# Routing weights normalised where they are gathered: a change to a transformer layer on one core

## What is computed

```python
x = x + 0.5 * ffn(layernorm(x))
x = x + attention(layernorm(x))
x = x + 0.5 * ffn(layernorm(x))

# in ffn: 2048 tokens, 64 experts, K = 4 of them per token, 32 slots per expert
logits = flat @ router_w.T
scores = softmax(logits)
_, topk_idx = top_k(logits + router_bias, K)
topk_w = take_along_axis(scores, topk_idx)
topk_w = topk_w / topk_w.sum(axis=-1, keepdims=True)
# tok_table, w_table: the first 32 tokens that chose each expert, and their weights
xg = flat[tok_table]
y = down(silu(gate(xg)) * up(xg))
out = zeros.at[tok_table].add(y * w_table)     # plus a shared expert of width 512
```

## Time and profile before

| | us |
|---|---|
| time, median of 3 runs | 971.72 |
| lowest and highest | 968.83, 972.66 |
| span of the profiled execution | 969.0 |
| TensorE busy | 918.5 (95%) |
| VectorE busy | 764.3 (79%) |
| ScalarE busy | 647.1 (67%) |
| GpSimd busy | 645.5 (67%) |

### The profile page before, as it was taken

One profiled execution on the slowest core, in us unless ns is written; L12 is line 12 of the kernel. 1 busy time (PEld: TensorE's weight loads), 2 busy tenths in 40 slices (PEclk: granted clock), 3 DMA queues, 4 the chain that ended last, 5 costly groups with the idle time before them and its releaser, 6 DMA issues.

```text
span 969.0 us, 18581 instructions
## 1 busy us (share of the span) xinstructions
PE 918.5 (95%) x5809; PEld 559.7 (58%) x5812; DVE 764.3 (79%) x2079; ACT 647.1 (67%) x1426; POOL 645.5 (67%) x607
## 2 busy tenths in 40 slices
PE   7989888999999999999999999999999999977987
PEld 4766465555555555555555555555555555765666
DVE  6954399998888888888888888888878789876247
ACT  5624546887777687777778778777777787643431
POOL 3367778878576868778676766867677455336642
PEclk9999999999999999999999999999999999989999
DMA  8979745566766878797885755756675574485657
GB/s 335 367 243 314 265 170 164 108 132 113 144 132 104 157 158 186 153 211 162 175 192 98 154 107 133 153 104 138 108 153 93 93 117 91 80 334 170 244 204 274
DMA packets 302978, 165.58 MB, mean 171 GB/s; under 512 B 278176, under 2 KB 285600, under 8 KB 300832
## 3 DMA queue, kind: packets, MB, share of 16 engines
q1 hardware_dynamic: 297696, 146.56, 62.8%
q0 software_dynamic: 3072, 9.44, 3.0%
q10 hardware_dynamic: 2112, 8.39, 2.2%
HBM read 68.93 MB, written 28.31 MB: 100 GB/s over the span
## 4 chain that ended last, share of the span: by engine, by line
PE 75%; DVE 13%; issue 4%; DMA 3%; ACT 3%; POOL 1%; SPq 0%; another core or an unknown queue 0%; ACTq 0%; DVEq 0%; POOLq 0%
PE b_o L110 5%; PE b_o L112 5%; PE b_o L111 5%; PE b_p L110 5%; PE b_s L110 5%; PE b_s L112 5%; PE b_s L111 5%; PE b_p L111 5%; PE b_p L112 5%; PE b_out L110 3%; PE b_out L112 3%; PE b_out L111 3%; PE b_v L110 2%; PE b_v L112 2%; PE b_v L111 2%
## 5 line engine op out<-in xcount | busy, mean ns | idle before, releaser
L2460 POOL TENSOR_TENSOR h<-pr,h 128x512 f16<-128x512 f32 x256 | 293.0, 1157 | 159.9 <-ACT h L1179 154.2
L1169 ACT ACTIVATE pr<-b_s,nmax,kappa 128x512 f32<-128x512 f32 x256 | 197.6, 774 | 42.2 <-DVE nmax L1915 37.0
L1912 DVE TENSOR_SCALAR_CACHE_REDUCE junk<-b_s 128x512 bf16<-128x512 f32 x256 | 175.3, 685 | 22.6 <-PE b_s L112 17.5
L1179 ACT ACTIVATE h<-pr 128x512 f16<-128x512 f32 x256 | 153.2, 626 | 0.8 <-DMA pT<-h 0.4
L1943 DVE SCALAR_TENSOR_TENSOR x<-b_out,rinv,x 128x256 f32<-128x256 f32 x256 | 111.4, 476 | 41.7 <-PE b_out L112 40.2
L110 PE MATMUL b_p<-xh,w 128*128 128x512 f16 x256 | 97.0, 379 | 4.3 <-DVE qT L1854 2.6
L110 PE MATMUL b_o<-pT,v 128*128 128x512 f16 x256 | 97.0, 379 | 1.7 <-DVE oT L1931 1.7
L110 PE MATMUL b_s<-kT,qT 128*128 128x512 f16 x256 | 97.0, 379 | 0.7 <-ACT pr L1169 0.7
L112 PE MATMUL b_s<-kT,qT 128*128 128x512 f16 x256 | 97.0, 379 | 0.0
L111 PE MATMUL b_s<-kT,qT 128*128 128x512 f16 x256 | 97.0, 379 | 0.0
L111 PE MATMUL b_o<-pT,v 128*128 128x512 f16 x256 | 97.0, 379 | 0.0
(11 more groups left out here) (225 smaller groups left out, 2236.6 us busy)
## 6 DMA issues: line engine op xcount, KB each, us to landing
raw<-in_experts SPq DMA_DIRECT2D x32, 768.0 KB, 7.2
raw_cs<-in_heads SPq DMA_DIRECT2D x16, 1024.0 KB, 5.1
zrows<-zero ACTq DMA_DIRECT2D x4, 2048.0 KB, 11.6
z<-zrows SPq DMA_DIRECT2D x16, 512.0 KB, 4.2
zrows<-zero SPq DMA_DIRECT2D x16, 512.0 KB, 4.0
zl<-zrows SPq DMA_DIRECT2D x16, 512.0 KB, 10.5
rows<-xn SPq DMA_DIRECT2D x8, 512.0 KB, 12.1
pT<-h SPq DMA_TRANSPOSE x256, 3.2
```

The source lines that it names most:

```text
L1169: act.activation(pr[n % 4][:], b_s[n % 3][:], ACT.Exp, bias=nmax[:, u % 2, i:i + 1], scale=kappa[:, s:s + 1], accum_out=rsum[:, u % 2, i:i ...
L1179: act.activation(h[n % 4][:, 0, :], pr[n % 4][:], ACT.Copy).then_inc(q["p_high"], 1)
L1912: dve.tensor_scalar(junk[n % 2][:], b_s[n % 3][:], 0.0, None, ALU.add, ALU.max, accum_out=peaks[:, n % 2:n % 2 + 1]).then_inc(q["peak_read ...
L2460: pool.tensor_tensor(h[n % 4][:, 1, :], pr[n % 4][:], h[n % 4][:, 0, :], ALU.subtract).then_inc(q["p_split"], 1)
```

## The change

The store of the weights follows the masked product at once: `sum_weights` and `weighted` are gone, with `esum` and `rsum_w`, two of the semaphores, and their places in the lists of VectorE and GpSimd. `slot_weights`, called once for each of the 32 groups, adds up all 64 gathered weights of each row (`whole`), takes the reciprocal (`fraction`), and multiplies the slot's own weight (`part`) by it. Three instructions on 128 rows are added to each call, with one more wait.

```diff
--- before.py
+++ after.py
@@ -148,8 +148,8 @@
         nmr = m.keep("nmr", [P, NT])
         best = m.keep("best", [P, NT, 8])
         mx = m.keep("mx", [P, NT])
-        esum = m.keep("esum", [P, NT])
-        rsum_w = m.keep("rsum_w", [P, NT])
+        whole, fraction = m.keep("whole", [P, NG]), m.keep("fraction", [P, NG])
+        part = m.keep("part", [P, NG])
         first = m.keep("first", [P, CAP])
         cand = m.keep("cand", [E, 2 * CAP])
         top = m.keep("top", [E, CAP])
@@ -235,7 +235,7 @@
         ctx.enter_context(nc.psum_tensor("all_banks", [P, 8 * 512], F32))
 
         names = ("consts p_hi p_lo veps_ready rstd_ready nmr_ready xn_ready xt_turned hi_done lo_done "
-                 "lgT_done lgT_sb pick_ready lg_done sh_done exp_done_w masked sum_ready w_ready w_out mask_ready maskT_done maskT_sb kidx_done keys_done "
+                 "lgT_done lgT_sb pick_ready lg_done sh_done exp_done_w w_ready w_out mask_ready maskT_done maskT_sb kidx_done keys_done "
                  "first_done cand_done top_done tab_done idx_ready gu_done sil_done hid_ready hhi_done hlo_done down_done x_added "
                  "turned sb_x act_done esil_done ehid_done h_turned sb_h y_done y_sb ws_ready x_done xp_done zp_chain stored "
                  "chain aw_in w_mul w_hi aw_ready bo_added s_done nmax_ready exp_done rinv_ready p_split p_high pv_done q_done "
@@ -1767,12 +1767,6 @@
                     dve.scalar_tensor_tensor(out=xs, in0=tb[o][:], scalar=0.5, in1=xs, op0=ALU.mult, op1=ALU.add
                                              ).then_inc(q["x_added"], 1)
 
-            def sum_weights(lap):
-                dve.wait_ge(q["masked"], lap + 1)
-                own.did(dve.tensor_reduce(esum[:], ex[:], X, ALU.add))
-                own.wait()
-                dve.reciprocal(rsum_w[:], esum[:]).then_inc(q["sum_ready"], 1)
-
             def rank_keys(lap):
                 dve.wait_ge(q["consts"], CONSTS)
                 for b in range(2):
@@ -1822,8 +1816,12 @@
                 if G >= 2:
                     dve.wait_ge(q["ws_ready"], G - 1)
                 own.did(dve.tensor_tensor(wtmp[s][:], xg[G % XGS][:, D:ROW], sel[:, 60 - EG * g:60 - EG * g + E], ALU.mult))
+                own.did(dve.tensor_reduce(whole[:, g:g + 1], xg[G % XGS][:, D:ROW], X, ALU.add))
                 own.wait()
-                dve.tensor_reduce(ws[:, g:g + 1], wtmp[s][:], X, ALU.add).then_inc(q["ws_ready"], 1)
+                own.did(dve.tensor_reduce(part[:, g:g + 1], wtmp[s][:], X, ALU.add))
+                own.did(dve.reciprocal(fraction[:, g:g + 1], whole[:, g:g + 1]))
+                own.wait()
+                dve.tensor_scalar(ws[:, g:g + 1], part[:, g:g + 1], fraction[:, g:g + 1], None, ALU.mult).then_inc(q["ws_ready"], 1)
 
             def expert_hidden(G):
                 s = G % 2
@@ -1984,7 +1982,6 @@
             first_keys(0)
             first_keys(1)
             first_keys(2)
-            sum_weights(0)
             hidden(4)
             first_keys(3)
             hidden(5)
@@ -2276,7 +2273,6 @@
             route(11)
             rank_keys(1)
             first_keys(0)
-            sum_weights(1)
             first_keys(1)
             hidden(21)
             first_keys(2)
@@ -2371,11 +2367,7 @@
             def masked(lap):
                 pool.wait_ge(q["exp_done_w"], lap + 1)
                 pool.wait_ge(q["mask_ready"], NCH * (lap + 1))
-                pool.tensor_tensor(ex[:], ex[:], mask[:], ALU.mult).then_inc(q["masked"], 1)
-
-            def weighted(lap):
-                pool.wait_ge(q["sum_ready"], lap + 1)
-                pool.tensor_tensor(ex[:], ex[:], rsum_w[:].unsqueeze(2).broadcast_to([P, NT, E]), ALU.mult).then_inc(q["w_ready"], 1)
+                pool.tensor_tensor(ex[:], ex[:], mask[:], ALU.mult).then_inc(q["w_ready"], 1)
 
             def gather(G):
                 lap, g = G // NG, G % NG
@@ -2539,7 +2531,6 @@
             scale_weights(0, 1)
             hidden_low(3)
             masked(0)
-            weighted(0)
             hidden_low(4)
             hidden_low(5)
             gather(0)
@@ -2728,7 +2719,6 @@
             hidden_low(18)
             masked(1)
             hidden_low(19)
-            weighted(1)
             hidden_low(20)
             hidden_low(21)
             gather(16)
```

## The result

The changed kernel takes 978.38 us (median of 4 runs, 976.43 to 981.89), the kernel before, measured beside it, 971.29: 1.0081 times the time, interval 1.0063 to 1.0100. It is slower by 7.1 us by the medians, 7.9 by the ratio, where 2.8 were forecast. Measured again beside some of the experiments it took 977.0 us, 1.0087 (1.0054 to 1.0121). I read both.

The account below looks back on a forecast made before the run. TensorE was taken as the bound, three quarters of the chain that ended last. -1.9 - 0.25 + 1.2 + 0.6 + 0.75 + 1.6 + 0.4 + 0.46 = +2.9 us, taken as 2.8: 974.5 us, range 969.5 to 978.0.

Parts of the forecast that it names:

- The gain, first lap: Ahead of the first gather, the removed sum and earlier store start the expert stage 1.9 us sooner.
- The gain, second lap: Ahead of the second lap's table, the removed sum of 1.4 us is mostly hidden; only 0.25 us is gained.
- The cost of one group: Each slot_weights call on VectorE takes 0.84 us instead of 0.38, 0.46 us more for each of 32 groups.
- No blocking of the new scaling: The one-column scaling in slot_weights isn't blocked by GpSimd; the rival, one blocked by 1.3 us, had 0.05.
- Where the cost is exposed, first lap: TensorE waits for longer slot_weights bunches: 1.2 us ahead of norm_qk(0) and 0.6 us at smaller places.
- norm_qk(0): First lap: groups 7 to 10 stand ahead of expert_hidden(8), for which this TensorE step waits; 1.2 us exposed.
- Three groups ahead of expert_hidden(2): First lap: estimated to expose half a group's cost to one; with group 14, 0.6 us in all.
- 11, 12 and 13 have idle time or a piece of gate_up behind them: First lap: these remaining groups, like 3 to 6, were taken as covered, with no cost counted.
- Second lap: Four places expose cost: 0.75 at expert_hidden(20), 1.6 at expert_hidden(23), 0.4 at expert_hidden(25), 0.46 us at group 31.
- The 0.75 at expert_in(21): Second lap: groups 19 and 20 ahead of expert_hidden(20) make TensorE's next step 0.75 us late.
- The carry through attention: A shift that TensorE shows at a stage's end passes through attention and the last stage in full.
- Rival 2, the falling clock: TensorE's clock falls in holes ahead of down(1) and behind gate_up(25): 976.2 us for one, 977.9 for both; chance 0.15.

Follow-up runs that it names:

- lap1_again: The change in the second lap alone, the first lap as in the kernel before: 1.0045 times the kernel before (1.0029 to 1.0061).
- before_spread: The kernel before with calls of slot_weights in both laps moved to where VectorE was idle: 971.12 us, 1.0006 (0.9995 to 1.0017).
- after_again: Profile of the whole changed kernel from its second measurement (977.0 us, 1.0087), its quickest execution: 974.08 us.
- after: Profile of the whole changed kernel from its first measurement (978.38 us, 1.0081), its slowest of four executions: 981.89 us.
- clear13: The changed kernel with GpSimd's three products beside group 13's product moved behind scatter(10): 977.09 us, 1.0063 of the kernel before.
- lap0_again: The change in the first lap alone, the second lap as in the kernel before: 1.0023 times the kernel before (1.0011 to 1.0034).
- late13: The changed kernel with slot_weights(13) moved behind expert_hidden(13) on VectorE: 977.82 us, 1.0058 of the kernel before.
- spread2: The changed kernel with the second lap's slot_weights calls moved away from the expert_hidden for which TensorE waits: 973.64 us, 1.0026 of the kernel before.
- added_again: The kernel before with the new, longer slot_weights and nothing removed: 979.65 us, 1.0093 of the kernel before (1.0075 to 1.0111).

## Why the prediction was wrong

The direction, and each mechanism that was named, held; the sum was 4 to 5 us short. Point by point:

- **The gain, first lap: right at its place, less in the time.** Gather(0) at 59.70 (forecast 59.5), turn group 0 at 64.28 (64.2). But in two profiles whose first lap is that of before, lap1_again and before_spread, that instruction comes 1.1 and 0.7 us earlier than in the profile on which I built, so part of the -1.9 was one slow gather in that execution. The runs give 1.6 us for both laps (0.5 to 2.6), where the forecast had 2.15.
- **The gain, second lap: -0.25.** No profile of the change shows it: table(1), less the shift at 863, moves by +0.05 (after_again), +1.2 (after), +0.5 (clear13), mostly where the granted clock is low for longer.
- **The cost of one group: right.** 0.83 or 0.84 against 0.38. **No blocking of the new scaling: right** as far as it was put to the test, which was once in the change's profile and in seven more scalings of the experiments' profiles (212 to 216 ns). The port rule of the Trainium skill's page SBUF — State Buffer, section "Who interferes with whom", had a second half that I did not weigh: a VectorE instruction with two SBUF inputs contends with a GpSimd one that reads SBUF. The trace agrees with it: 4.24 us for group 13's product, and clear13 takes it away. It bears on the *old* product, which the change only moves later. The kernel before had such a row already, group 19's 2.16 us at 893.07, and I didn't read it.
- **Where the cost is exposed, first lap: the step that failed.** Forecast 1.8; the profiles of after_again and lap0_again have 4.7 and 3.5 from turn group 0 to 147.89 (about 1.1 of after_again's is a fall of the clock at 71 us), and the runs of lap0_again 2.2 net of the gain, so about 4. norm_qk(0) was right: in lap0_again the shift goes from -1.2 at 79.14 us to -0.1, 1.1 where 1.2 was forecast. "Three groups ahead of expert_hidden(2)" was mis-sized: TensorE's expert_in(3) lost 1.1, nearly all of 3 x 0.46, where the forecast had half a group to one; 0.5 of it was won back by 79 us. And "11, 12 and 13 have idle time or a piece of gate_up behind them" was false in effect: +1.2 by turn group 13, 0.9 of it in one step there, which clear13 and late13 both take away. The added work alone was covered (before, `ehid` of group 13 begins 3.3 us ahead of its turning); it moved the old product under GpSimd's three. Another 0.5 followed behind it (group 14 and 15), as forecast.
- **Second lap: sizes right, a little low.** In after_again the four steps are 0.9, 1.5, 0.6 and 0.4, where 0.75, 1.6, 0.4 and 0.46 were forecast, 3.4 for 3.2. The runs of lap1_again have 4.4 (2.8 to 5.9). spread2 shows that it is these places that pay. The 0.75 at expert_in(21) came out right on a row that a blocked product had made: in clear13's profile, where group 19's isn't blocked, there is no such step.
- **The carry through attention: right on the mean** (+0.1 over the nine profiles of the table), with up to 1.8 us of variation either way in an execution.
- **Rival 2, the falling clock, is part of it, and it doesn't decide.** I had two holes in view; neither profile of the change has a fall there. The fall at 112 us came at a third, behind group 13 to 15, and after has another behind the wait ahead of expert_in(21) (0.57 from 904 to 908 us), which after_again, with a wait of 0.84 us there, has not. Over all runs of the change the time at the lower clock is 22.5 us per execution (8 runs; span x 2 x (1 - mean clock)), of the kernel before beside after_again 18.2. At half speed 4.3 us more can cost 2.1 at most. lap0_again has 18.8 beside 19.4 before, and costs 2.2 us with no more time at the lower clock; lap1_again has 22.4 beside 19.4, up to 1.5 of its 4.4. Between the two profiles of the change it matters more: 27 us at the lower level in after, 14 in after_again, and 7.8 us of time between them.
- **The range** ended at 978.0 because the unknown in it was the price of a group. The price was known to 0.01. The unknown was how many of the 32 groups stand on the path: I had 19 (20 by my own list), and took all others as covered from the idle time behind them in one execution. The 978.38 of the first measurement lie only 0.4 above the range, less than the clock's share can be; that the sum was short by 5 us is clear of that.

Added up from the halves: 2.2 + 4.4 = 6.6, of 7.9 (6.1 to 9.7) by the change's ratio. In the first lap the terms are -1.9 of gain and 1.1 - 0.5 + 1.1 + 1.2 + 0.5 at the places, 1.5 for the 2.2 of the runs. In the second they are 3.4 at the places and about 1 for which I have only the clock: the shift at table(1) and turn group 23 in executions whose clock is low there. That last share is argued and not shown.

## What to carry to other kernels

Work added to an engine that idles for half of a stage (before, VectorE was busy 42% of 50 to 112 us and 50% of 866 to 931 us) is not paid by its share of idle time, but place by place: for each bunch of added operations find the next instruction of that engine that another engine takes, and count the whole bunch unless the idle time behind it is there in more than one execution. A road shortened once gains once; a cost put into 32 groups is paid at each place where it sticks out, and in full as soon as the cover is gone. Before moving a VectorE product of two SBUF tiles, look at what GpSimd does at its new time, and look for rows of it that are long already; and where work must go in, put it between the products that wait for ScalarE, which here gave back about two thirds of the cost by order alone.

## What was not expected of the hardware

- A product of two SBUF tiles on VectorE that takes 0.22 us stood 4.24 us through three GpSimd products in a row, recorded as starting 0.6 us ahead of the first of them; even one of 2 columns stood 1.92 us. The few reductions and one-column scalings that had a GpSimd product beside them (3 and 8 in all profiles) kept 0.21 or 0.22 us. GpSimd's gathers and scatters blocked nothing: 16 of the changed kernel's products ran inside one, none over 0.23 us.
- Chips ran the kernel before at 971 us (three) and at 1000 us (one), with granted clocks of 0.990 to 0.992 and of 0.974, and gave the parts of the change 0.9984 and 1.0093 on the former, 0.9954 and 1.0058 on the latter. The changed and old kernels must share a chip.
- Two executions of the changed kernel differed by 7.8 us with 14 and 27 us at the lower clock, and two of added_again, on one chip, by 11.5 us with 21 and 45: the falls are not fixed by the program.
